# Score matmuls of latent attention on one half of the array's rows

## The reference

```
scores = einsum('bqhd,bkhd->bhqk', qq, kk) / sqrt(8)
scores = where(causal, scores, finfo.min)
probs  = softmax(scores);  y = einsum('bhqk,bkhd->bqhd', probs, v)
```

## Time and profile before

| | |
|---|---|
| median of 3 runs | 499.88 us |
| profiled execution, first to last instruction (span) | 498.5 us |
| TensorE matmuls busy | 438.1 us, 88%, 4044 instructions |
| weight loads busy | 232.8 us |
| VectorE busy | 364.8 us, 73% |
| ScalarE busy | 264.8 us, 53% |
| GpSimd busy | 63.9 us, 13% |
| DMA | 20.05 MB in 21124 packets |

### The profile page before, as it was taken

The page is one execution under the profiler, slowest core; times in us unless marked ns, Lnnn a source line. Parts: engine busy times, 40 slices in busy tenths (PEclk is TensorE's granted clock), DMA queues, the critical chain, the costliest instruction groups (busy, mean ns, idle before and its releaser), DMA issues.

```text
span 498.5 us, 10894 instructions
## 1 busy us (share of the span) xinstructions
PE 438.1 (88%) x4044; PEld 232.8 (47%) x4044; DVE 364.8 (73%) x1049; ACT 264.8 (53%) x486; POOL 63.9 (13%) x56
## 2 busy tenths in 40 slices
PE   2667569899999999999999997899998999987995
PEld 2323233345445356354545544454545545654653
DVE  6566288388767887796768785667687775788886
ACT  5236247545876663778865375776543444221110
POOL 7233002433000220110002030000010000010000
PEclk9997599899999999999999998999999999999898
DMA  6037300016600124700001355000400000000000
GB/s 202 9 75 157 43 2 2 3 34 151 103 3 3 34 46 88 122 3 2 3 2 22 71 122 75 3 3 2 130 1 3 2 1 23 1 21 1 1 21 22
DMA packets 21124, 20.05 MB, mean 40 GB/s; under 512 B 2856, under 2 KB 19752, under 8 KB 20680
## 3 DMA queue, kind: packets, MB, share of 16 engines
q1 hardware_dynamic: 21072, 19.36, 18.7%
HBM read 10.70 MB, written 7.47 MB: 36 GB/s over the span
## 4 chain that ended last, share of the span: by engine, by line
PE 52%; DVE 27%; issue 7%; DMA 5%; ACT 4%; SPq 3%; POOL 1%; DVEq 0%; ACTq 0%; POOLq 0%
PE bank_A L1071 7%; PE bank_c L1034 6%; PE bank_A L1000 6%; PE bank_B L1020 5%; PE bank_M L1082 5%; DVE x L943 4%; DMA q_stack<-in_c_rows 4%; DVE k_diag L923 4%; DVE k_diag L928 3%; PE bank_B L1115 3%; PE bank_M L986 3%; PE bank_M L1089 2%; DVE differences L819 2%; SPq L468 2%; PE bank_A L1121 2%
## 5 line engine op out<-in xcount | busy, mean ns | idle before, releaser
L672 ACT ACTIVATE p_mla<-bank_B 128x512 f32<-128x512 f32 (+1 forms) x176 | 97.4, 561 | 78.9 <-PE bank_B L1023 77.1
L819 DVE CUSTOM_DVE_ANT_0 differences<-masks,bank_A 128x384 bf16<-128x384 bf16 (+1 forms) x128 | 78.4, 612 | 18.7 <-PE bank_A L1000 13.4
L651 ACT ACTIVATE pT_loc<-sT_loc 32x512 f32<-32x512 f32 x136 | 85.1, 625 | 4.5 <-DVE sT_loc L846 3.1
L1000 PE MATMUL bank_A<-k_stack,q_stack 128*128 128x128 bf16 (+3 forms) x256 | 70.1, 307 | 14.5 <-DMA q_stack<-in_c_rows 8.0
L1020 PE MATMUL bank_B<-q_stack,k_stack 128*128 128x512 bf16 (+3 forms) x256 | 67.9, 302 | 1.0 <-DVE k_diag L923 0.8
L1115 PE MATMUL bank_B<-xrT,k_diag 128*128 128x512 f32 x128 | 63.7, 612 | 3.7 <-DVE k_diag L923 3.2
L839 DVE TENSOR_REDUCE row_max<-bank_A 128x16 f32<-128x512 f32 (+1 forms) x36 | 24.8, 690 | 39.4 <-PE bank_A L1071 39.2
L1071 PE MATMUL bank_A<-k_diag,qT 128*32 128x512 f32 x272 | 49.7, 757 | 0.0
L1023 PE MATMUL bank_B<-masks 128*128 128x128 bf16 x256 | 49.1, 219 | 0.0
L1000 PEld LDWEIGHTS bank_A<-k_stack,q_stack 128*128 128x128 bf16 x256 | 25.6, 100 | 49.9 <-issue 26.4
L1034 PE MATMUL bank_c<-p_mla,v_mla 128*9 128x128 f32 (+3 forms) x512 | 47.0, 437 | 1.4 <-ACT p_mla L672 1.4
(11 more groups left out here) (137 smaller groups left out, 624.8 us busy)
## 6 DMA issues: line engine op xcount, KB each, us to landing
parts_dram<-parts SPq DMA_DIRECT2D x16, 192.0 KB, 2.7
k_stack<-parts_dram SPq DMA_DIRECT2D x8, 384.0 KB
q_stack<-parts_dram SPq DMA_DIRECT2D x8, 384.0 KB
parts_dram<-parts SPq DMA_DIRECT2D x16, 128.0 KB, 2.7
k_diag<-kT SPq DMA_DIRECT2D x64, 18.0 KB
x<-in_x SPq DMA_DIRECT2D x4, 256.0 KB, 7.6
parts_dram<-parts SPq DMA_DIRECT2D x16, 64.0 KB, 2.3
out<-x SPq DMA_DIRECT2D x4, 256.0 KB, 2.2
```

What stands on the lines that cost most here:

```text
L651: last = nc.scalar.activation(pT_loc[rows, :, rows], sT_loc[rows, t % 2, :].rearrange("p (h k) -> p h k", h=H), ACT.Exp, scale=SCALE)
L672: drained_by(nc.scalar.activation(p_mla[:, n % P_RING, m:m + len(heads), j * P:], src, ACT.Exp, scale=SCALE), step)
L819: drained_by(nc.vector.tensor_tensor_reduce(differences[:, 0:w], masked16[:, S - w:], bank[:, 0:w], -1.0, -NEG, ALU.add, ALU.min, dst), step)
L1000: last = nc.tensor.matmul(bank[:, n * w:(n + 1) * w], q_stack[b % 2][:, h // 2, h % 2, i * P:(i + 1) * P], k_stack[b % 2][:, h // 2, 0:w], ...
```

## The change

Heads 0 to 7 get slot 0 (rows 0 to 63), heads 8 to 15 slot 1 (rows 64 to 127): head h is at column group h % 8 of slot h // 8. The weights are ordered accordingly. A score matmul then addresses the 50 rows of its head's slot alone, and nothing of the other slot has to be zero: `q_stack` loses its second version, `clear` goes, and with it the semaphore `zeroed`. A mask must be in the same rows as the score that it is added to: it becomes two matmuls over 64 rows, one with the upper and one with the lower half of the identity and of the causal tile, of which one has 128 columns and the other 64, since the rest is zero. All score matmuls of a unit come first, then its masks; only the first has the start flag. The groups go in order 0, 2, 1, 3 in S and in E, so that neighbouring groups are in different halves. A group's shift rows go in by one DMA instead of two. The mask table in SBUF grows by four tiles.

```diff
+GROUP_ORDER = [0, 2, 1, 3]
 def score_units():
-    for g in range(H // 4):
+    for g in GROUP_ORDER:
...
+def halves(square):
+    return np.tile(np.concatenate([square[0:SLOT], square[SLOT:]], axis=1), (2, 1))
...
-        q_stack = [sb(f"q_stack{i}", [P, H // 2, 2, S], BF16) for i in range(2)]
+        q_stack = [sb(f"q_stack{i}", [P, H // 2, S], BF16) for i in range(2)]
...
-                            dst = q_stack[b % 2][rows, :, hp, :] if side else k_stack[b % 2][rows, :, :]
+                            dst = q_stack[b % 2][rows, :, :] if side else k_stack[b % 2][rows, :, :]
...
-                        sp.dma_start(q_stack[b % 2][row:row + 2, :, hp, :],
+                        sp.dma_start(q_stack[b % 2][row:row + 2, :, :],
                                      rows_dram[2:4, :].rearrange("o (a n) -> o a n", n=S)).then_inc(stacks_in, 16)
...
-                    for hp in range(2):
-                        row = SLOT * hp + SHIFT_ROW
-                        src = shift_dram[b, g].rearrange("r (e a i) n -> e r a (i n)", e=2, i=NT)[hp]
-                        sp.dma_start(q_stack[b % 2][row:row + 2, 2 * g:2 * g + 2, hp, :], src).then_inc(shift_in[g], 16)
+                    row, a0 = SLOT * (g // 2) + SHIFT_ROW, 4 * (g % 2)
+                    sp.dma_start(q_stack[b % 2][row:row + 2, a0:a0 + 4, :],
+                                 shift_dram[b, g].rearrange("r (a i) n -> r a (i n)", i=NT)).then_inc(shift_in[g], 16)
...
-            def clear(i):
-                nc.gpsimd.memset(k_stack[i][:].bitcast(F32), 0.0)
-                nc.gpsimd.memset(q_stack[i][:].bitcast(F32), 0.0).then_inc(zeroed, 1)
-                pool.wait_ge(zeroed, i + 1)
-
-            clear(0)
...
-                if step == ("MB", 1, 0):
-                    clear(1)
...
+                    half_rows = slice(SLOT * (heads[0] // 8), SLOT * (heads[0] // 8) + SLOT)
+                    rows = slice(half_rows.start, half_rows.start + STACK_ROWS)
                     for n, h in enumerate(heads):
                         last = nc.tensor.matmul(bank[:, n * w:(n + 1) * w],
-                                                q_stack[b % 2][:, h // 2, h % 2, i * P:(i + 1) * P],
-                                                k_stack[b % 2][:, h // 2, 0:w], start=True, stop=i >= 2,
+                                                q_stack[b % 2][rows, h % 8, i * P:(i + 1) * P],
+                                                k_stack[b % 2][rows, h % 8, 0:w], start=n == 0, stop=i >= 2,
                                                 skip_group_check=True)
-                        if i < 2:
-                            last = nc.tensor.matmul(bank[:, (n + 1) * w - P:(n + 1) * w], eye16, causal16,
-                                                    start=False, stop=True, skip_group_check=True)
+                    for n in range(len(heads) if i < 2 else 0):
+                        for low in range(2):
+                            c = (n + 1) * w - P + low * SLOT
+                            last = nc.tensor.matmul(bank[:, c:(n + 1) * w], half_eye[half_rows, low, :],
+                                                    half_causal[half_rows, low, low * SLOT:], start=False, stop=True,
+                                                    skip_group_check=True)
...
                     for m, h in enumerate(exp_units(g, j)[u]):
-                        nc.tensor.matmul(bank[:, m * w:(m + 1) * w], k_stack[b % 2][:, h // 2, j * P:(j + 1) * P],
-                                         q_stack[b % 2][:, h // 2, h % 2, j * P:], start=True, stop=False,
+                        nc.tensor.matmul(bank[:, m * w:(m + 1) * w], k_stack[b % 2][rows, h % 8, j * P:(j + 1) * P],
+                                         q_stack[b % 2][rows, h % 8, j * P:], start=m == 0, stop=False,
                                          skip_group_check=True)
-                        last = nc.tensor.matmul(bank[:, m * w:m * w + P], eye16, causalT16,
-                                                start=False, stop=True, skip_group_check=True)
+                    for m in range(len(exp_units(g, j)[u])):
+                        for low in range(2):
+                            last = nc.tensor.matmul(bank[:, m * w:m * w + SLOT * (low + 1)], half_eye[half_rows, low, :],
+                                                    half_causalT[half_rows, low, 0:SLOT * (low + 1)],
+                                                    start=False, stop=True, skip_group_check=True)
```

More of the change, by code:

```diff
@@ L51 @@
 SHIFT_ROW = TERMS * HD
+STACK_ROWS = SHIFT_ROW + 2
 P_RING = 2
@@ L129, in maxima @@
         steps = []
-        for g in range(H // 4):
-            steps += [("S", b, u) for u in range(PER_GROUP * g, PER_GROUP * g + PER_GROUP)] + [("SHIFT", b, g)]
+        for n, g in enumerate(GROUP_ORDER):
+            steps += [("S", b, u) for u in range(PER_GROUP * n, PER_GROUP * n + PER_GROUP)] + [("SHIFT", b, g)]
         return steps
@@ L234, in constants @@
         "c_eye": eye,
-        "c_masks": as_bf16(np.concatenate([eye, causal, causal.T, pair, np.zeros((P, S - P), np.float32), causal],
-                                          axis=1)),
+        "c_masks": as_bf16(np.concatenate([eye, halves(eye), halves(causal), halves(causal.T), pair,
+                                           np.zeros((P, S - P), np.float32), causal], axis=1)),
         "c_rope": np.stack([np.tile(np.repeat(t, H // 2, axis=0), (2, 1)) for t in (cosT, sinT)], axis=1),
@@ L268, in build @@
         eye = sb("eye", [P, P])
[L269 to L272, removed]
+        masks = sb("masks", [P, 7 * P + 512 + S], BF16)
+        eye16, pair16 = masks[:, 0:P], masks[:, 7 * P:7 * P + 512]
+        half_eye, half_causal, half_causalT = (masks[:, P * n:P * n + 2 * P].rearrange("p (r c) -> p r c", r=2)
+                                               for n in (1, 3, 5))
+        masked16 = masks[:, 7 * P + 512:]
         rope = sb("rope", [P, 2, S])
@@ L363, in build @@
         pT_cleared = sem("pT_cleared")
-        zeroed = sem("zeroed")
         diag_zeroed = sem("diag_zeroed")
@@ L491, in _ @@
                     _, b, g = step
-                    n = b * (H // 4) + g
+                    n = b * (H // 4) + GROUP_ORDER.index(g)
                     wait_drained(sp, step)
@@ L676, in _ @@
                     act.wait_ge(pv_done, pv_no[step])
-                    if b and g == 0:
+                    if b and g == GROUP_ORDER[0]:
                         wait_full(act, ("X1", b - 1))
@@ L771, in _ @@
                     wait_full(dve, step)
-                    ku, qu, rq = (bank[:, 64 * n:64 * n + 64].rearrange("p (a e d) -> p e d a", e=2, d=HH) for n in range(3))
-                    rk = w_ropek.rearrange("p (a e) d -> p e d a", e=2)
+                    ku, qu, rq = (bank[:, 64 * n:64 * n + 64].rearrange("p (e a d) -> p e d a", e=2, d=HH) for n in range(3))
+                    rk = w_ropek.rearrange("p (e a) d -> p e d a", e=2)
                     part = HH // 2
@@ L821, in _ @@
                     else:
-                        dst = neg_max[:, g, :, a0:a0 + len(heads) // 2, i].rearrange("p e a -> p a e")
-                        src = src.rearrange("p (a e) k -> p a e k", e=2)
+                        dst = neg_max[:, g, m:m + len(heads), i]
                         drained_by(nc.vector.tensor_reduce(dst, src, AX.X, ALU.max, negate=True), step)
                 elif kind == "SHIFT":
-                    n = b * (H // 4) + step[2]
+                    n = b * (H // 4) + GROUP_ORDER.index(step[2])
                     wait_full(dve, step)
@@ L1009, in _ @@
                     g = step[2]
-                    wait_drained(pe, ("S", b, PER_GROUP * (g + 1) - 1))
+                    wait_drained(pe, ("S", b, PER_GROUP * (GROUP_ORDER.index(g) + 1) - 1))
                     wait_free(pe, step)
                     full_by(nc.tensor.transpose(bank_of(step)[0:4 * NT, 0:P],
-                                                neg_max[:, g].rearrange("p e a i -> p (e a i)"), eye[:]), step)
+                                                neg_max[:, g].rearrange("p a i -> p (a i)"), eye[:]), step)
                 elif kind == "E":
```

13 lines of the change are left out of this document (7 added, 6 removed).

## The result

| | before | after |
|---|---|---|
| median of the runs side by side | 499.88 us (496.96 to 500.12) | 517.2 us (514.04 to 520.41) |
| ratio, 95% interval | | 1.036 [1.030, 1.042] |
| profiled execution, its time / its span | – / 498.5 us | 514.96 / 513.0 us |

The change makes the kernel 3.6% slower. The forecast was 527 (500 to 552). The four runs of after lie further apart than those of before; in the order of their times their mean granted clocks are 0.968, 0.963, 0.954 and 0.950.

The account below looks back on a forecast made before the run. TensorE was taken as the bound, 95% busy from 100 to 430 us. 36.9 - 2 - 4.2 - 1.6 - 1.6 = +27.5 on a 498.5 span, plus 1.4 around it, gave 527 us; range 500 to 552.

Parts of the forecast that it names:

- changes of array shape: TensorE, between half-row S or E steps and whole-array steps: 215 new changes at 0.125 us, 26.9 us before the 0.95 share.
- Its two largest terms: On TensorE: 26.9 us for changes of shape and 11.9 us for added mask matmuls, together 36.9 at a 0.95 share.
- the overlap: Neighbouring S and E steps in opposite halves, 43 pairs, partly running at once on TensorE: -2 us, between 0 and -4.
- stack loads: Query stack loads in 8 KB instead of 1 KB runs: -1.6 us for batch 0 and -1.6 for batch 3.
- the free change of shape: Rival: changing rows on TensorE costs nothing, leaving the mask cost less the gains, 502 us; chance 10%.
- the doubled masks: TensorE: each of 384 masks becomes two matmuls, 0.031 us more each, 11.9 us before the 0.95 share.
- the signs named beforehand: Trace signs: for, L786 1.1 us, transposes near 10.8, first score near 49; against, E starting before S's last turn ends.
- zeroing: Opening: without GpSimd's memsets VectorE's four normalisations take 1.11 instead of 5.33 us, -4.2 us.
- query stack in long runs, twice: Query stack loads for batches 0 and 3, in 8 KB instead of 1 KB runs: -1.6 us each.
- clock: TensorE at 1.2 of 2.4 GHz around the stack-load wait; a shorter wait may leave less of it; left out of the sum.
- halves run side by side: Rival: at 43 opposite-half S/E pairs the shorter step disappears, 17 us, with no gaps: 487 us; chance 8%.
- The slow loads of halves: Rival: TensorE weight loads of a half no longer hide, mask pairs cost 40 us instead of 11.9: 556 us; chance 12%.

Follow-up runs that it names:

- experiment 3: The kernel before with a second 64-column mask matmul, adding zeros over all 128 rows, behind each of the 384 masks: 507.49 us, 1.018 of before.
- experiment 1: The kernel after with the groups in order 0, 1, 2, 3 and nothing else changed: 509.65 us, against 517.2 of after.
- experiment 4: The kernel after with each mask as one 128-column matmul over all 128 rows, scores still on half of the rows: 524.22 us, 1.050 of before.
- experiment 2: The kernel before with GpSimd's first zeroing of both stacks delayed until VectorE has written the normalised x and its scaled copy: 494.43 us, 0.991 of before.
- experiment 9: The kernel after with the zeroing of both stacks and its semaphore put back: 520.40 us, 1.043 of before.
- experiment 7: The kernel before with the query stack's two versions one behind the other, so rows are written in 8 KB runs: 499.19 us, 1.000 of before.
- experiment 11: The kernel after with groups in order 0, 1, 2, 3 and 62 S or E steps moved one place earlier: 519.53 us, 1.038 of before.

## Why the prediction was right, and where it wasn't

The bound was read rightly: where TensorE has no slack, added matmuls and gaps are time. So was the mechanism that decides: changes of array shape cost time, and more of it than anything else in the change. The sum was 10 us too high (+27.5, measured +17.3 by the medians). Its two largest terms were too large and the overlap too small, which all pull one way; 3.2 us for stack loads, of which at most 1 came, pull the other, and that is luck. The range of 500 to 552 was wide enough to hold the free change of shape as well (502), so it is the experiments and not the range that tell the two apart.

On the ruler the doubled masks are +2.55 (experiment 3) and the early starts -1.0 (1.5 us at the rate of experiment 1); of +8.8 that leaves 7.2 us for 75 more changes of shape (189 against 114), 0.097 each. Experiment 4 gives 0.087 by another way. Of the signs named beforehand those for the forecast came (normalisations 1.12 us, first transposes at 10.46, first score at 48.37), and one against it as well: second steps start before the first one's turn is over. They do so at 40 of 133 borders, too few to outweigh the rest. Term by term over the whole kernel:

| term | predicted | shown |
|---|---|---|
| doubled masks | +11.3 | +8.7 (experiment 3) |
| changes of shape | +25.6 (0.125 each) | +19 to +21 where nothing hides them (0.087 to 0.097 each) |
| overlap of opposite halves | -2 (0 to -4) | -5 to -7.5: early starts of 7.5 us; 67 more such borders bring 4.9 on the ruler, 7.5 by the medians (experiment 1) |
| zeroing | -4.2 | -4.4 in before, -3.2 in after (experiments 2, 9) |
| query stack in long runs, twice | -3.2 | 0 (experiment 7) |
| clock | left out | -2.0 in the opening, +3.7 behind the load, -1.7 at 95 us, +1.2 behind batch 3's load: +1.2 in these two executions |

- **Changes of shape** were right as a mechanism and over-sized. The 0.127 behind the 64-row transposes misled me; the whole-to-column gap of 0.10 was the better row, and it was my lower end. The Trainium skill ("TensorEngine Tiling (Array Packing)", Key Properties) says that changing the tiling mode drains the engine; the runs agree with it in that each change costs 0.087 to 0.097 us.
- **Overlap** was too small because I took mostly the last mask as shareable. A 512-column score disappears whole, as at 127.57. The Trainium skill ("TensorE: Matmul & The Clock Gate", Why this matters for your kernels) has matmuls on distinct row groups start within 4 ns; here the records stand 0.01 us apart. The rival "halves run side by side" had the right physics; it needed gaps of nothing, and these are 0.1.
- **Masks** cost 0.030 where they stand, and 76% of that in the sum, not 95%: the busy share says how much idle time there is, not how much of it lies behind the added instructions.
- **Stack loads**: I read the rate of 150 GB/s as that of 1 KB runs. With 8 KB runs the wait is the same. In after the way from the first key load's issue to the first score is 11.3 us against 12.3, and 12.4 in experiment 7. Over all traces it is 11.2 to 12.05 in the kernels on half rows and 12.0 to 12.45 in the others; that part of a us has no cause here.
- **The clock** I named and left out. Since it rose at 61 us in both traces, a first score 6.9 us earlier bought less than 6.9. It need not be so: in experiment 2, with the first score at 52.35, it was back by 58, and in experiment 4, with 48.29, by 51.9. What decides it is open.
- **The zeroing** was right in size. VectorE's four instructions end just behind the fill in before and in experiment 9, so it is the fill's end that they wait for.
- The slow loads of halves (556) are dead: a half's bf16 load takes 94 or 95 ns against 98.

```profile
L1031 PEld LDWEIGHTS bank_B<-masks 64*128 64x128 bf16 x512 | 39.8, 95 | 14.3 <-issue 0.2
```

With the zeroing at -4.5, the shorter way of the stacks at -1.0 and the clock at +1.2, the terms shown add up to between +16 and +20 on a span that grew 14.5. So 1 to 6 us of them fell into idle time outside the landmarks: in 60 to 100 us, and behind 298 us, where TensorE had 7 and 9 us of slack. That is inferred, no run isolates it.

## What to carry to other kernels

Count the changes of array shape along TensorE's order, and price each at 0.09 to 0.1 us (measured here at full clock); a matmul on fewer rows saves nothing by itself. In these kernels it paid only where its neighbour in the program was on the other half (the neighbour always wrote another bank as well; what the bank does, no run shows). So count which steps really stand side by side: here the order made for that had 43 such borders, the plain one 110. Don't buy fewer changes by reordering a list whose results arrive just in time; and look what GpSimd fills beside VectorE before you redesign to get rid of the fill: moving it gave the 4.4 us without the 20 that the changes of shape cost. And before a few us between two traces are explained, compare where TensorE ran at half speed in each.

## What was unexpected of the hardware

- A fill by GpSimd beside VectorE's fp32 subtract-and-multiply makes it 4.8 times as long (5.33 against 1.12 us for four). With a fill half as long it is 3.62 (experiment 9), and both times VectorE is done 0.14 us behind the fill's end.
- Two neighbouring steps on opposite halves of the rows overlap at 101 of 110 borders without anything in the program asking for it, and on the same half at none of 23 (experiment 1).
- Half-speed stretches stand behind the wait for the stacks in every trace, but their length differs between kernels with nearly the same instructions (2.7 us in experiment 7, 3.6 in experiment 4, about 5 in experiment 2, 13.1 in after, and over 16, with a second one behind it, in experiment 11), and in the half-row kernels run time follows the mean granted clock: 514.0 at 0.968, 520.4 at 0.950. In before, 0.972 and 0.975 came with 497.1 and 500.3.
